# Loads and stores issued from ScalarE's queue, three row buffers in each lane, and image 2's group norm products behind the scores

## The reference

```python
# layer 0
h = group_norm(x, 32 groups, eps 1e-5, gn_w, gn_b)
q, k, v = split(qkv_w @ h + qkv_b)                 # 128 channels each
attn = softmax(q^T k * C**-0.5)                    # 1024 x 1024 per image
x1 = x + proj_w @ (v attn^T) + proj_b
# layer 1
q, k = Wq @ x1 + bq, Wk @ x1 + bk                  # 16 channels each
v = Wv @ x1 + bv
y = gamma * (v softmax(q^T k)^T) + x1
```

## Time and profile before

| | us |
|---|---|
| median of 3 runs | 1585.69 (1584.01 to 1586.72) |
| the profiled execution | 1587.17 |
| its span, first to last instruction | 1585.0 |
| TensorE busy, weight load busy | 1483.5, 1120.0 |
| VectorE, ScalarE, GpSimd busy | 1284.3, 1214.9, 1238.6 |
| mean granted clock of TensorE | 0.987 of full speed |
| moved by DMA | 305.22 MB, mean 193 GB/s |

### The profile page before, as it was taken

The page is one execution under the profiler, slowest core; times in us unless marked ns, Lnnn a source line. Parts: engine busy times, 40 slices in busy tenths (PEclk is TensorE's granted clock), DMA queues, the critical chain, the costliest instruction groups (busy, mean ns, idle before and its releaser), DMA issues.

```text
span 1585.0 us, 43920 instructions
## 1 busy us (share of the span) xinstructions
PE 1483.5 (94%) x16777; PEld 1120.0 (71%) x16777; DVE 1284.3 (81%) x2508; ACT 1214.9 (77%) x1698; POOL 1238.6 (78%) x1027
## 2 busy tenths in 40 slices
PE   5799999999999989999999999999999999999977
PEld 2567777767777767776777777777777677767756
DVE  6678888877888878887888888878888788878885
ACT  3578877877787878877878778878878788778874
POOL 4788878878888878787888878888888788788653
PEclk9899999999999999999999999999999999999999
DMA  1999999999999999999999999999999999999999
GB/s 49 164 164 195 202 200 197 203 193 202 187 203 203 202 197 200 196 195 200 206 196 200 202 194 200 202 200 198 201 196 198 206 193 199 197 199 195 191 194 183
DMA packets 1081438, 305.22 MB, mean 193 GB/s; under 512 B 1068272, under 2 KB 1068944, under 8 KB 1081232
## 3 DMA queue, kind: packets, MB, share of 16 engines
q1 hardware_dynamic: 1080080, 302.41, 110.2%
q10 hardware_dynamic: 1152, 0.00, 0.0%
HBM read 17.13 MB, written 16.78 MB: 21 GB/s over the span
## 4 chain that ended last, share of the span: by engine, by line
SPq 47%; PE 29%; DVE 7%; DMA 7%; ACT 5%; issue 4%; POOL 1%; DVEq 0%; ACTq 0%; POOLq 0%
SPq L304 44%; DMA pt<-rows 6%; PE mixed L816 4%; PE mixed L818 4%; PE mixed L817 4%; PE scores L771 3%; DVE nmax L565 3%; DVE rows L582 3%; PE scores L773 2%; PE scores L772 2%; PE scores L801 2%; SPq L295 2%; ACT rows L473 2%; PE bank_w L890 2%; PE bank_w L882 1%
## 5 line engine op out<-in xcount | busy, mean ns | idle before, releaser
L565 DVE TENSOR_REDUCE nmax<-scores 128x1 f32<-128x1024 f32 x512 | 620.4, 1217 | 149.8 <-PE scores L801 131.4
L816 PE MATMUL mixed<-v_head,pt 128*128 128x129 f16 x4096 | 719.6, 222 | 3.4 <-DMA pt<-rows 3.1
L817 PE MATMUL mixed<-v_tail,pt 128*128 128x128 f16 x4096 | 718.9, 219 | 0.0
L818 PE MATMUL mixed<-v_head,pt 128*128 128x129 f16 x4096 | 718.8, 220 | 0.0
L366 POOL TENSOR_TENSOR rows<-prob,rows 128x1024 f16<-128x1024 f32 x256 | 545.3, 2130 | 21.4
L361 POOL TENSOR_SCALAR rows<-prob 128x1024 f16<-128x1024 f32 x256 | 267.5, 1045 | 265.8 <-ACT prob L460 161.0
L465 ACT ACTIVATE scores<-scores,nmax 128x1024 f32<-128x1024 f32 x256 | 278.9, 1089 | 183.7 <-DVE nmax L565 183.1
L817 PEld LDWEIGHTS mixed<-v_tail,pt 128*128 128x128 f16 x4096 | 406.0, 99 | 3.1
L816 PEld LDWEIGHTS mixed<-v_head,pt 128*128 128x128 f16 x4096 | 399.5, 98 | 5.4 <-DMA pt<-rows 4.6
L818 PEld LDWEIGHTS mixed<-v_head,pt 128*128 128x128 f16 x4096 | 397.1, 97 | 0.0
L582 DVE SCALAR_TENSOR_TENSOR rows<-scores,rows 128x1024 f16<-128x1024 f32 x256 | 312.9, 1222 | 78.4 <-ACT rows L473 78.2
(11 more groups left out here) (110 smaller groups left out, 1923.0 us busy)
## 6 DMA issues: line engine op xcount, KB each, us to landing
x_raw<-in_x_dram SPq DMA_DIRECT2D x32, 512.0 KB, 4.6
out_dram<-y SPq DMA_DIRECT2D x64, 256.0 KB, 3.2
pt<-rows SPq DMA_TRANSPOSE x512, 5.1
w_qkv<-in_L_conv_qkv_w_dram SPq DMA_DIRECT2D x3, 64.0 KB, 4.1
b_qk<-in_L_conv_bk_dram SPq DMA_DIRECT2D x8, 0.1 KB, 2.3
b_qk<-in_L_conv_bq_dram SPq DMA_DIRECT2D x8, 0.1 KB, 1.9
w_proj<-in_L_conv_proj_w_dram SPq DMA_DIRECT2D x1, 64.0 KB, 4.9
w_v<-in_L_conv_Wv_dram SPq DMA_DIRECT2D x1, 64.0 KB, 4.7
```

The costliest lines, as they stand in the source:

```text
L565: nc.vector.reduce_max(nmax[l][:, tile.i % TILES:tile.i % TILES + 1], scores[l][:, :], AX.X, negate=True).then_inc(maxed[l], 1)
L816: mm(mixed[l][:, 0:C + 1], head, vh[:, p, m, 0:C + 1], start=(m == 0), stop=False)
L817: mm(mixed[l][:, 0:C], head, vt[:, p, m, :], start=False, stop=False)
L818: done = mm(mixed[l][:, 0:C + 1], tail, vh[:, p, m, 0:C + 1], start=False, stop=(m == TILES - 1))
```

## The change

Loads of images 3 to 31 and all stores are issued by ScalarE, at the end of its slot. SyncE keeps the loads of images 0 to 2, which are now all issued before the first slot, and the transposes. The load of image 3 moves from slot 0 to slot 3. `rows` holds three tiles in each lane, and a head waits for the transpose of the tile three before. The two group norm products of image 2 alone go behind the scores of their slot. One small VectorE instruction of the setup (`gam_bv`) moves from `setup_fold` (after slot 0) to `setup_v` (after slot -6), with the counts of its semaphore adapted.

```diff
+ROWS = 3
-LOADS = Steps(-16)
-LOADS_LEFT = -11
+LOADS = Steps(-16, first={3: (-13,)})
+GN_BEHIND = 2
-        rows = [sb(f"rows{l}", [C, 2, 2, N], F16) for l in range(2)]
+        rows = [sb(f"rows{l}", [C, ROWS, 2, N], F16) for l in range(2)]
-        def two_before(tile):
-            return LANES[tile.lane][tile.i - 2] if tile.i >= 2 else None
+        def rows_before(tile):
+            return LANES[tile.lane][tile.i - ROWS] if tile.i >= ROWS else None
 @block.sync
             def body(slot):
-                for im, _ in LOADS.at(slot):
-                    load_x(im)
                 if tile := TILE_AT[0].get(slot - SWING[0]):
                     swing(tile)
-                for im, h in STORE.at(slot):
-                    store_y(im, h)
                 if tile := TILE_AT[1].get(slot - SWING[1]):
                     swing(tile)
...
+            load_first(2)
+            every_slot(body, 0)
 @block.scalar
+            def load_x(im):
+                act.wait_ge(x_biased, im.n - X_BUFS + 1)
+                act.wait_ge(h32_done, im.n - X_BUFS + 1)
+                act.wait_ge(h_head_done, im.n - X_BUFS + 1)
+                act.dma_start(x_raw[:, im.n % X_BUFS, :], x_img[im.n]).then_inc(x_loaded[im.n % X_BUFS], 16)
+
+            def store_y(im, h):
+                act.wait_ge(y_done, im.n * TILES + PER_HALF * (h + 1))
+                act.dma_start(out_img[im.n, :, h * HALF:(h + 1) * HALF], y[:, h, :]).then_inc(y_stored[h], 16)
             def body(slot):
...
                 for im, _ in H_HEAD.at(slot):
                     h_head_out(im)
+                for im, _ in LOADS.at(slot):
+                    if im.at_least(X_BUFS):
+                        load_x(im)
+                for im, h in STORE.at(slot):
+                    store_y(im, h)
 @block.vector
             def setup_v():
...
+                nc.vector.tensor_tensor(gam_bv[:, :], gam[:, :], b1_v[:, :], ALU.mult).then_inc(setup_dve, 1)
             def setup_fold():
...
-                nc.vector.tensor_tensor(gam_bv[:, :], gam[:, :], b1_v[:, :], ALU.mult).then_inc(setup_dve, 1)
 @block.tensor
             def body(slot):
                 for im, step in GN.at(slot):
-                    gn_product(im, step)
+                    if im.n != GN_BEHIND:
+                        gn_product(im, step)
...                                                  # the scores of the next slot
+                for im, step in GN.at(slot):
+                    if im.n == GN_BEHIND:
+                        gn_product(im, step)
```

More of the change, by code:

```diff
@@ L266, in build @@
         B_LOADS, B1_LOADS, W_LOADS = 6, 16, 4
-        DVE_QK, DVE_B_Q, DVE_V, DVE_FOLD, DVE_BIAS, DVE_QK1, DVE_ALL = 4, 5, 7, 9, 10, 12, 20
+        DVE_QK, DVE_B_Q, DVE_V, DVE_FOLD, DVE_BIAS, DVE_QK1, DVE_ALL = 4, 5, 8, 10, 11, 12, 20
         def swings(tile):
@@ L284, in _, with load_first @@
             col = lambda v: v.rearrange("(p a) -> p a", a=1)
[L286 to L295, removed]
+            def load_first(n):
+                sp.dma_start(x_raw[:, n, :], x_img[n]).then_inc(x_loaded[n], 16)
             def swing(tile):
@@ L304, in swing @@
                 sp.dma_start_transpose(pt[l][:, i % RING, :, :],
-                                       rows[l][:, i % 2, :, :].rearrange("p s n -> p (s n)")
+                                       rows[l][:, i % ROWS, :, :].rearrange("p s n -> p (s n)")
                                        ).then_inc(swung[l][i % RING], 16)
             def body(slot):
-                for im, _ in LOADS.at(slot):
-                    load_x(im)
                 if tile := TILE_AT[0].get(slot - SWING[0]):
                     swing(tile)
-                for im, h in STORE.at(slot):
-                    store_y(im, h)
                 if tile := TILE_AT[1].get(slot - SWING[1]):
                     swing(tile)
-            load_x(Image(0))
+            load_first(0)
             for j in range(3):
                 sp.dma_start(w_qkv[:, j, :], qkv_w[j * C:(j + 1) * C, :]).then_inc(w_qkv_loaded, 16)
-            load_x(Image(1))
+            load_first(1)
             for dst, src in ((w_proj[:, :], proj_w), (w1_v[:, :], Wv), (w1_qk[0:CQK, :], Wq),
@@ L328, in _ @@
                     sp.dma_start(b1_qk[r * CQK:(r + 1) * CQK, h:h + 1], col(src)).then_inc(b1_loaded, 16)
-            every_slot(body, LOADS_LEFT)
+            load_first(2)
+            every_slot(body, 0)
             for h in range(2):
@@ L357, in head_row0 @@
                 stand_apart()
-                if early := two_before(tile):
+                if early := rows_before(tile):
                     pool.wait_ge(swung[0][early.i % RING], swings(early))
                     stand_apart()
-                nc.gpsimd.tensor_scalar(rows[0][:, tile.i % 2, 0, :], prob[:, tile.i % 2, :], 1.0, 1.0, ALU.mult,
+                nc.gpsimd.tensor_scalar(rows[0][:, tile.i % ROWS, 0, :], prob[:, tile.i % 2, :], 1.0, 1.0, ALU.mult,
                                         ALU.mult).then_inc(row_headed[0], 1)
@@ L365, in tail_row0 @@
                 pool.wait_ge(row_headed[0], tile.i + 1)
-                nc.gpsimd.tensor_tensor(rows[0][:, tile.i % 2, 1, :], prob[:, tile.i % 2, :],
-                                        rows[0][:, tile.i % 2, 0, :], ALU.subtract).then_inc(row_tailed[0], 1)
+                nc.gpsimd.tensor_tensor(rows[0][:, tile.i % ROWS, 1, :], prob[:, tile.i % 2, :],
+                                        rows[0][:, tile.i % ROWS, 0, :], ALU.subtract).then_inc(row_tailed[0], 1)
             def gn_root_out(im):
@@ L469, in head_row1 @@
             def head_row1(tile):
-                if early := two_before(tile):
+                if early := rows_before(tile):
                     act.wait_ge(swung[1][early.i % RING], swings(early))
                 act.wait_ge(exped[1], tile.i + 1)
-                nc.scalar.activation(rows[1][:, tile.i % 2, 0, :], scores[1][:, :], ACT.Copy,
+                nc.scalar.activation(rows[1][:, tile.i % ROWS, 0, :], scores[1][:, :], ACT.Copy,
                                      scale=P_UP).then_inc(row_headed[1], 1)
+            def load_x(im):
[6 more added lines that the diff above has]
+                act.dma_start(out_img[im.n, :, h * HALF:(h + 1) * HALF], y[:, h, :]).then_inc(y_stored[h], 16)
             def norm(tile):
@@ L581, in tail_row1 @@
                 dve.wait_ge(row_headed[1], tile.i + 1)
-                nc.vector.scalar_tensor_tensor(out=rows[1][:, tile.i % 2, 1, :], in0=scores[1][:, :], scalar=P_UP,
-                                               in1=rows[1][:, tile.i % 2, 0, :], op0=ALU.mult,
+                nc.vector.scalar_tensor_tensor(out=rows[1][:, tile.i % ROWS, 1, :], in0=scores[1][:, :], scalar=P_UP,
+                                               in1=rows[1][:, tile.i % ROWS, 0, :], op0=ALU.mult,
                                                op1=ALU.subtract).then_inc(row_tailed[1], 1)
```

## The result

The changed kernel takes 1568.8 us in the median of 4 runs (1566.4 to 1575.8) against 1585.3; the ratio is 0.9913 with an interval of 0.9892 to 0.9935. Run again beside other kernels it gave 0.9921 (0.9891 to 0.9951). By the ratio it is faster by 14 us, with 10 to 17 in the interval; the medians differ by 16. The forecast was 39 us. Its sign is right and its size is off by more than twice; the measured time lies outside its own range of 1534 to 1562 as well. Three executions of the later runs, two of the kernel before and one of an experiment, took 2847 to 2965 us; they stand in no ratio here.

The account below looks back on a forecast made before the run. Two close bounds, TensorE's work and the transfer stream: 35 us from the stream's period, 2 from the fill and 2 from the drain make 39 us, so 1546 against 1585.7 us; own range 1534 to 1562.

Parts of the forecast that it names:

- the stream's new period: Transfer time per image in the main part: falls from 47.9 to 46.5 us, gaining 35 us over 25 periods.
- The holes: SyncE's transpose queue: a copy there lets the DMA engines run dry, 16 GB/s in one half microsecond against a mean of 199.
- rival A: DMA engines: copies cost the same from any queue, period stays near 47.9 us, 1582 us in all; chance 0.14.
- The neighbour that misled: Stretch after the last load: 45.97 us an image, taken as TensorE's own pace, with SyncE's queue keeping up.
- Three buffers: Heads' wait for a transpose: the third row buffer removes it, but alone is worth nothing where the stream is the bound.
- ScalarE's queue: End of ScalarE's slot: each copy's issue takes 0.5 us, mostly covered by 0.64 us a slot of waiting for the row maximum.
- Rival B: ScalarE becomes the bound because issues beside transposes hold it longer: 1626 or 1683 us; chance 0.14.
- The fill: Kernel's start: a 6.37 us wait goes, later row maxima take part back; 2 us gained, between 6.4 gained and 3 lost.
- The drain: Kernel's end, from 1515 us: three stores leave SyncE's queue between its last transposes; 2 us gained, between 0 and 3.4.

Follow-up runs that it names:

- the two phases with copies: SyncE transposes by themselves, no computation: 128 alone, then with 8 loads and 16 stores from SyncE, then from ScalarE; alone 318.1 us, copies adding 31 and 33 us.

## Why the prediction was wrong

**The step that failed** is the stream's new period: "I take 46.5", from bounds of 45.1 and 47.9, on the ground that a copy makes holes and that these close when it comes from another queue. Measured were 47.4. That term was 35 us and is 25 x (47.90 - 47.40) = 12.5 us. The holes are real, but by themselves the copies take the same time from the transposes out of either queue. So rival A describes the transfers themselves, and the rule that I had cited beside it (the Trainium skill, "DMA: Bandwidth & Descriptors", section "Issuing engines are not separate DMA queues") agrees with the two phases with copies: 2.73 us a transpose with the copies in SyncE's queue and 2.75 with the copies from ScalarE, against 2.49 alone. In the kernel the queue is worth something for the loads alone, 14 us with the stores beside them and 19 without. Why is open: the queue of the three phases never rests either, and there it is worth nothing.

**What the stream costs** can be estimated without the holes, from the phases alone: 16 transposes of 2.49 us are 39.8; the copies 3.9 to 4.2; fetches 137 x 47.9 / 1585 = 4.1 an image by 0.8 us, 3.4 us. Together 47.1 with the copies from SyncE and 47.4 with the copies from ScalarE. The trace of after has 47.4. The kernel before has 47.9, so the sum fits only the changed kernel: some 0.8 us an image, which go with the loads in SyncE's queue, are in no term of it. I had read the transposes' pace as waiting for "the engines below" and looked at the copies alone; the fetches, nearly as large, were on the page (137 packets in q8) and not in my sum.

**The neighbour that misled.** I took the stretch without loads for TensorE's own pace and for proof that the stream keeps up. The products of q and k are all in it; what it lacks are the two small group norm products, which I named and put at nothing. They are busy for 7.0 us in 25 images, 0.28 us each, about the 0.30 that is missing: TensorE's pace is 46.27, not 45.95 (45.97, to be exact), and with loads gone the stream just keeps up (22 us faster, no waits at `attend`). So the room was 1.6 us an image and not 1.95. Of it the change won 0.5; the other 1.1 go with the loads' bytes, which it doesn't touch.

**Three buffers.** "Alone, worth nothing" held only where the loads stand in SyncE's queue. Beside loads from ScalarE it was 8 us. No trace shows by what: that stalls of a stream and a TensorE that run almost level (47.4 and 46.3) add up is my guess. The period of the one trace with two buffers does not bear it out.

**ScalarE's queue.** Right, and better than forecast: 0.35 us an issue, no wait behind it. Rival B is gone.

**The fill.** The direction of each part was right, the sum not: the scores of slot 3 come at 52.97 for 51.57, +1.4 us where I had -2, and the first inversion at 60.12 for 59.07. In a second trace of the changed kernel both are at the level of before (51.54 and 59.04). The late load is worth 6.5 us at the scores of slot 3 (45.05 in the kernel before with that edit), and the order of the products takes 8 back in this trace, of which I had 4.5; the half clock was missing. Some of this comes back later: the 65th inversion is 1.8 us earlier than before. **The drain**: I had 2 us. From the 449th inversion to the last it takes 180.8 us after and 178.1 before, so nothing was won there. Together, 1.8 + 24 x 0.51 - 2.7 = 11.3 us, the difference of the two profiled spans.

**Smaller things.** The nine TensorE lines of rows 1 come to 25% and not 24; nothing hangs on it. Rival A, at 0.14, had the better picture of the transfers, and its time of 1582 us missed too, by 13 us.

## The version to keep

The changed kernel with the products ahead of the scores: 1565.8 us, 0.9876 (0.9858 to 0.9894) of the kernel before; with the stores back in SyncE's queue it is no different (0.9879).

## What to carry to other kernels

When a queue never rests, ask whether its instructions take time of their own or wait for what is below, and time the stream by itself, alone and with its neighbours, before a saving in the queue is counted; it took one run here. That run tells what the transfers cost, and not yet what the queue costs inside the kernel. A stretch with less work tells a bound only if all that it lacks is known. An order that puts a small product behind large ones is paid by the in-order engine that reads it.

## What was not expected of the hardware

- A 16 KB fetch of TensorE's instructions costs the stream of transposes 0.8 us: 39 fetches 32 us, 10 fetches 8 us, with TensorE equally busy, and a standstill behind each. In this kernel that would be some 110 us of transfer time, an estimate, 137 x 0.8.
- Copies cost a stream of transposes by itself about the same from its own queue and from another, 3.9 and 4.2 us for 1 MB.
- Cutting a load in four costs 21 us in the transposes' queue, in part perhaps because its last piece comes late.
- Left open: why 64 stores cost nothing in SyncE's queue, with a median issue of 0.78 us each, when 29 loads of 0.5 us cost 14 to 19 us there. What the traces do show is that the stores' time is no extra: with the stores in SyncE's queue (loads on ScalarE) its 64 store issues take 53 us, and its transposes' issues 58 us less than in the changed kernel (1345 for 1402). With the loads there instead, the transposes give back 6 us only (1397).
